# One accumulating DMA in place of two VectorE additions in the rotary step of a 32-item attention pipeline

## The reference

```python
def _rope(x, sin, cos):
    xe = x[..., ::2]
    xo = x[..., 1::2]
    re = xe * c - xo * s
    ro = xe * s + xo * c
    return jnp.stack((re, ro), axis=-1).reshape(x.shape)

def _attn(xq, ctx, wq, wkv, wo, bo):
    q = _heads(xq @ wq)
    k, v = jnp.split(ctx @ wkv, 2, axis=-1)
    ...
    q = _rope(q, sq, cq)
    k = _rope(k, sk, ck)
    sim = jnp.einsum('bhnd,bhmd->bhnm', q, k) * DH ** (-0.5)
    a = jax.nn.softmax(sim, axis=-1)
    o = jnp.einsum('bhnm,bhmd->bhnd', a, v)
```

## Time and profile before

| what | value |
|---|---|
| median of 3 runs | 428.16 us (425.07 to 430.17) |
| profiled execution | 422.87 us, of which the span on the core is 420.7 us |
| granted TensorE clock, mean | 0.984 of full speed |
| busy share of the span | PE 91%, DVE 74%, ACT 72%, GpSimd 39% |
| sum on DVE (L691) | 64 times, 44.4 us in all |
| sine on GpSimd (L281) | 64 times, 82.0 us in all |

### The profile page before, as it was taken

One profiled execution on the slowest core, in us unless ns is written; L12 is line 12 of the kernel. 1 busy time (PEld: TensorE's weight loads), 2 busy tenths in 40 slices (PEclk: granted clock), 3 DMA queues, 4 the chain that ended last, 5 costly groups with the idle time before them and its releaser, 6 DMA issues. The chain is left out here.

```text
span 420.7 us, 9918 instructions
## 1 busy us (share of the span) xinstructions
PE 383.0 (91%) x3599; PEld 288.5 (69%) x3599; DVE 312.4 (74%) x677; ACT 303.6 (72%) x1042; POOL 165.6 (39%) x159
## 2 busy tenths in 40 slices
PE   7778989999999999999999989899798898898976
PEld 3446767777877777777767577777586686687554
DVE  4699898988887999988999477764567567567430
ACT  2376777886885878787868947797698778688722
POOL 4578593523643443733346241321473402002020
PEclk9899999999999999999999999999999989989989
DMA  6334424232252121212221010000000000000000
GB/s 189 119 131 127 157 89 163 83 115 96 74 191 107 64 89 68 85 63 90 75 77 68 34 51 2 2 2 0 2 2 2 3 2 2 2 2 2 2 25 26
DMA packets 16036, 26.11 MB, mean 62 GB/s; under 512 B 3614, under 2 KB 6308, under 8 KB 15860
## 3 DMA queue, kind: packets, MB, share of 16 engines
q1 hardware_dynamic: 13572, 18.43, 12.2%
q0 software_dynamic: 1696, 6.16, 5.1%
q10 hardware_dynamic: 720, 0.87, 0.7%
HBM read 8.15 MB, written 0.52 MB: 21 GB/s over the span
## 5 line engine op out<-in xcount | busy, mean ns | idle before, releaser
L281 POOL TENSOR_TENSOR swp<-swp,small 128x512 f32<-128x512 f32 x64 | 82.0, 1293 | 108.2 <-PE bank L873 76.5
L411 ACT ACTIVATE prob<-bank,nmax 128x128 f32<-128x128 f32 x256 | 91.5, 391 | 4.8 <-DVE nmax L668 4.8
L506 ACT ACTIVATE raw<-bank,nmax 128x128 f32<-128x128 f32 x256 | 73.5, 391 | 20.1 <-DVE nmax L772 20.1
L772 DVE TENSOR_REDUCE nmax<-bank 128x4 f32<-128x512 f32 x64 | 41.2, 686 | 26.5 <-PE bank L873 26.3
L411 ACT ACTIVATION_READ_ACCUMULATOR prob<-bank,nmax 128x1 f32 x256 | 59.3, 231 | 0.0
L668 DVE TENSOR_REDUCE nmax<-bank 128x4 f32<-128x512 f32 x64 | 41.2, 685 | 17.7 <-PE bank L873 17.6
L222 POOL TENSOR_TENSOR rstd<-vare,neg_half 128x4 f32<-128x4 f32 x12 | 12.4, 1034 | 104.5 <-DVE vare L613 104.4
L675 DVE TENSOR_TENSOR prob<-prob,rz 128x512 f32<-128x512 f32 x64 | 49.9, 780 | 2.2
L873 PE MATMUL bank<-hT,wqkv 128*128 128x512 f32 x96 | 50.0, 606 | 1.1 <-ACT hT L394 1.1
L417 ACT ACTIVATE probT<-bank 128x512 f32<-128x512 f32 x32 | 19.1, 597 | 40.4 <-PE bank L958 40.4
L873 PE MATMUL bank<-km,q 32*128 32x128 f32 x512 | 37.5, 284 | 10.7 <-ACT raw L506 6.1
(11 more groups left out here) (112 smaller groups left out, 649.3 us busy)
## 6 DMA issues: line engine op xcount, KB each, us to landing
swp<-raw SPq DMA_DIRECT2D x128, 128.0 KB, 2.1
wqkv<-in_wqkv POOLq DMA_DIRECT2D x13, 192.0 KB, 3.0
wo<-in_wo POOLq DMA_DIRECT2D x2, 512.0 KB, 5.1
wff<-in_wff POOLq DMA_DIRECT2D x1, 1024.0 KB, 5.6
wsq<-in_wsq POOLq DMA_DIRECT2D x1, 576.0 KB, 6.2
x<-in_x SPq DMA_DIRECT2D x2, 256.0 KB, 4.6
wmod<-in_wmod POOLq DMA_DIRECT2D x1, 512.0 KB, 4.2
out_x<-x SPq DMA_DIRECT2D x2, 256.0 KB, 2.3
```

The costliest lines, as they stand in the source:

```text
L281: nc.gpsimd.tensor_tensor(four(swp[:, m % 2, f, :]), four(swp[:, m % 2, f, :]), sin[f], ALU.mult).then_inc(rope_sin[f], 1)
L411: last = nc.scalar.activation(prob[:, hh, bcols(u)], S[hh][:, bcols(u)], ACT.Exp, bias=nmax[:, s % 2, hh, u:u + 1], accum_out=zsum[:, s % ...
L506: last = nc.scalar.activation(prob1[:, s % 2, hh, bcols(u)], SB[(2 * s + hh) % 3][:, bcols(u)], ACT.Exp, bias=nmax[:, s % 2, hh, u:u + 1])
L772: nc.vector.tensor_reduce(nmax[:, s % 2, hh, :], four(SB[(2 * s + hh) % 3][:, :]), AX.X, ALU.max, negate=True).then_inc(rowmax1[hh], 1)
```

## The change

1. `rope_sum` leaves DVE. GpSimd now issues, after its two sines of an item, one DMA that adds `swp` onto `qk` for queries and keys together (128 partitions by 1024 fp32, 512 KB read from `swp`, added onto 512 KB of `qk`). It waits for both cosines and both sines of the item first.
2. `roped` is now one semaphore for each buffer (even and odd items) that the DMA raises by 16. `score(s)` and `swap(m)` wait for it.
3. GpSimd no longer waits for `scores[0]` ahead of its sines.

```diff
@@ sync: swap(m)
                     if m >= 2:
-                        sp.wait_ge(roped[f], m - 1)
+                        sp.wait_ge(roped[m % 2], 16 * (m // 2))
@@ gpsimd
+            def rope_sum(m):
+
+                for f in range(2):
+                    pool.wait_ge(rope_cos[f], m + 1)
+                    pool.wait_ge(rope_sin[f], m + 1)
+                pool.dma_start(qk[:, m % 2, :, :], swp[:, m % 2, :, :], accum_op=ALU.add).then_inc(roped[m % 2], 16)
...
             def l0_slot(s):
-                if 0 <= s < ITEMS - 2:
-                    pool.wait_ge(scores[0], s + 1)
                 if s + 1 < ITEMS - 1:
                     rope_sine(s + 1, 0)
                     rope_sine(s + 1, 1)
+                    rope_sum(s + 1)
                 loads(s)
                 background0(s)
@@ gpsimd: background0(s)
                 if s == 29:
                     rope_sine(ITEMS - 1, 0)
                     rope_sine(ITEMS - 1, 1)
+                    rope_sum(ITEMS - 1)
@@ vector
-            def rope_sum(m, f):
-                dve.wait_ge(rope_sin[f], m + 1)
-                dve.wait_ge(rope_cos[f], m + 1)
-                nc.vector.tensor_tensor(qk[:, m % 2, f, :], qk[:, m % 2, f, :], swp[:, m % 2, f, :], ALU.add).then_inc(
-                    roped[f], 1)
...
-                if s + 1 < ITEMS:
-                    rope_sum(s + 1, 0)
-                    rope_sum(s + 1, 1)
                 if s + 2 < ITEMS:
                     rope_cosine(s + 2, 0)
@@ tensor: score(s)
+                pe.wait_ge(roped[s % 2], 16 * (s // 2 + 1))
                 for f in range(2):
-                    pe.wait_ge(roped[f], s + 1)
                     if s:
                         pe.wait_ge(exps[f], s)
```

## The result

The changed kernel takes 502.71 us in the median of 4 runs (496.11 to 508.13); the kernel before, beside it, 426.62. The ratio is 1.1785, with a 95% interval from 1.1695 to 1.1876: 76 us slower. The forecast was 476.7 us, with a range to 520.

What follows compares the result with a forecast made beforehand. TensorE was taken as the bound in plain slots, with VectorE's sums hidden; the new DMA closes a loop. 422.87 + 45.2 + 4.6 - 1.3 = 471.4 us profiled, 476.7 at the median, 5.3 above; range 438 to 520.

Steps and rivals of the forecast that it cites:

- T: Shortest first-layer slot, around the loop scores, row maxima, cosine, DMA, next scores: 3.08 + 0.3 + L, forecast at 8.98 us.
- L: Time of the new accumulating DMA from issue to landing, taken as 5.6 us, ends of the range 3.9 and 7.2.
- (a): Rival: the addition's second read is nearly free, L about 3.9, 439.2 us at the median; chance 0.11.
- (b): Rival: the DMA is hidden, L about 3.2, +4.2 us, at the edge of no change; chance 0.06.
- (c): Rival: faster, the DMA lands in about as little as a swap, 2.1 us, giving -4.3 us; chance 0.03.
- (d): Rival: much slower, L above 7.2, an addition at a fraction of the copy rate, 523 us at 7.2; chance 0.10.
- +45.2 us for 28 intervals: First layer, scores to next scores up to item 28: 27 intervals grow to 8.98 us, one already 9.07.
- a sign of being wrong: First-layer slots: the sine, not the cosine, closes the loop, making slots longer than 3.4 us plus the landing.
- The start: Item 0's first scores wait for the new DMA, coming at 23.05 and not 18.44: +4.6 us.
- The end: Item 31's sum, last before its scores, is done a slot sooner by DMA: 1.3 us off.
- The wait for the scores: Removing GpSimd's wait for scores[0] ahead of its sines: put at nothing, though sines could collide with VectorE's work.
- The clock: TensorE, busy some 6.7 of 9 us in first-layer slots: no drop in granted clock worth a term.

## Why the prediction was right, and where it was off

**The bound and the direction.** Right. VectorE's time had no value in plain slots, and the DMA closed a loop that the sum had closed with 1.28 us. All versions with the DMA in the path are slower. The range held the time, but it reached from 438 to 520, and the forecast for the change, +49 us, was two thirds of the 76 measured.

**The loop's length.** T was 3.08 + 0.3 + L = 8.98 us with L = 5.6. In slots closed by the cosine it was 8.55 in the slot shown. L was 4.8 there and 5.2 in the median, so 5.6 was too high. The allowance of 0.3 us was too small: from the cosine to the start of the DMA alone 0.6 us pass. The two errors nearly cancel, by luck: 3.08 + 0.6 + 5.2 = 8.9 us.

**The cost of an addition.** Twice a copy's engine time was the right size: forecast 2.9 and 1.5 us, measured 2.85 and 1.35. Rivals (a), (b) and (c), with a second read that is nearly free, are refuted by the plain copy; (b)'s landing of 3.2 us is that of the copy (3.0), not of the addition (5.2). The Trainium skill's figure for a plain DMA ("DMA: Bandwidth & Descriptors", anatomy of one DMA), about 3.2 us by its formula (an estimate), fits that copy's 3.0. The chosen rule, equal bytes read, fits the addition. Rival (d), L above 7.2, is out too: the longest landing was 6.1.

**The step that was mis-sized: +45.2 us for 28 intervals, measured +69.0.** By the prediction's own sum the 15 intervals up to item 15 were to grow by 18.6 us and grew by 42.2; the 13 after it were to grow by 26.5 and grew by 26.8. So all that is missing lies where weight loads are still issued. (That the 13 agree so well is in part luck: five of their DMAs were released by a sine.) The argument took T from the cosine's loop and carried over the swaps' 2.1 us, so that the sine came 1.6 to 2.5 us into its slot, before the cosine. But the new DMA is issued just before the queries' swap of the next item and holds it up: 6.11 us in the chain shown, 3.6 in the median. Then both sines are late, and 15 of 32 DMAs were released by them. The prediction had named this as a sign of being wrong, with slots longer than 3.4 us plus the landing, and for nearly half the slots it came true. The prediction had put the swaps' time into L ("fall into the same time") and never L's time into the swaps. In the early slots weight loads share the engines (5.5 us to landing, from 3.0), and swaps land in 4.1 us in the median where they land in 3.5 later; that this is why those slots suffered the most isn't tested by itself. That opening the cosine's loop gave just 7 us shows the second path, and the 27 us of traffic beside the path show the price of traffic. The plain copy shows the step most sharply: the prediction let the wait cost nothing below L = 3.3, and rival (b) had +4.2 us for L = 3.2. The copy landed in 3.0 and cost 29 us (1.069).

**The start.** +4.6 forecast, +5.5 measured. Right.

**The end.** -1.3 forecast, +0.8 measured for the last three intervals. The last scores came 6.53 us after those before, as against 6.32, with no wait shown ahead of them, so the sum's 1.28 us weren't won; what took their place isn't shown.

**The wait for the scores.** Put at nothing: 1.0024 in the old kernel. In the new one its removal saved 13 us: with it the sines end behind the cosine in every slot, and release all 32 DMAs. The collision that the prediction feared is real (VectorE's multiplications of two tiles take 56.9 us and not 49.9 without the wait, the sums on VectorE), but costs no time while VectorE has room; with traffic it did.

**The clock.** "No drop worth a term" was wrong on the drop (0.86 and 0.91). On the term it was right for the second stretch, where the kernel with filled waits has the clock back and not the time; for the first stretch it stays open.

**GpSimd's queue.** Right for the changed kernel. The issue took 0.89 us, not the 0.6 of the loads, and no one waited for it; the version with four issues an item ran into it.

## What to carry to other kernels

Here an operation of 1.28 us on an engine with room cost nothing, while the same work as a DMA cost its latency wherever a loop closed through it. Before moving a step, list every input that it waits for and go round each loop once with the new latency. A new transfer must also be priced as traffic: ask which transfers are issued in the microseconds after it, who waits for those, and take their landing longer. Bytes decide that too, and the addition here counted its bytes twice (2.85 us of the engines against 1.35). Check the forecast by stage: here the sum was right where nothing else moved on the DMA engines but swaps, and less than half of what came where weight loads did.

## What the runs showed of the hardware

- An accumulating DMA of fp32 from GpSimd landed in 2.9 us for 128 KB (64 partitions), 3.4 for 256 KB and 5.2 for 512 KB; a plain copy of 512 KB in 3.0. In engine time the 512 KB cost 2.85 us of all 16 engines against 1.35.
- GpSimd needs 0.89 us to issue the addition, 0.59 for the copy, and some 0.5 to 0.6 us pass before the DMA starts when its input has just been released.
- A 128 KB swap from another queue, issued 1.1 us after the addition, took 6.11 us instead of 2.1. With traffic beside the path the swaps' median hardly moved (2.4), their longest landing rose from 6.0 to 8.3 us, and the time rose by 27 us.
- A VectorE multiplication of two tiles in core memory took 3.68 us beside two sines on GpSimd, which read and write core memory, where 0.69 is usual.
